# Two mixture-of-experts stages in a twelve-stage fp32 kernel: three of four token groups go from every expert to their two chosen ones, by sorted blocks and indexed transfers

## The chip, the core and the metric

The kernel runs on one core of a Trainium2 chip. The time is the device time of one launch, in microseconds (us). Engines are named as in the profile: PE (matrix products), DVE, ACT and POOL (element-wise work, POOL also issues indexed transfers), SP (issues DMAs). Names that end in q are the queues that feed them.

## The reference, cut to what matters

The state x has 2 x 1024 tokens of 128 numbers. Twelve stages in a row each add to x a function of its layer norm: L0 ffn, L0 attention, L0 ffn, L1 ffn, L1 attention, L1 ffn, L2 ffn, L2 attention (a time mixing of two layers), L2 ffn, L3 ffn, L3 attention, L3 ffn. The change is mainly about the two L1 ffn stages, called the L1 mixtures here:

```python
scores = xf @ gate_w                                   # 2048 tokens, 8 experts
top_v, top_i = jax.lax.top_k(scores, TOP_K)            # TOP_K = 2
probs = jax.nn.softmax(top_v, axis=-1)
combine = jnp.zeros((t, e), dtype=xf.dtype).at[jnp.arange(t)[:, None], top_i].add(probs)
h = jax.nn.gelu(jnp.einsum('td,edf->etf', xf, w1) + b1[:, None, :], approximate=False)   # 128 -> 512
y = jnp.einsum('etf,efd->etd', h, w2) + b2[:, None, :]                                   # 512 -> 128
out = jnp.einsum('etd,te->td', y, combine)
```

Six of eight entries in a row of `combine` are zero. The L2 and L3 mixtures have the same form with 256 in place of 512.

## The kernel before

x stays in SBUF the whole time as 16 tiles of 128 tokens; four tiles make a group (`NG` = 4 groups). The program of each engine is written stage after stage by hand, with semaphores between them; nothing is scheduled by a tool. All weights are in SBUF before the mixtures start, except those of L3, which SP loads into L1's place once the second L1 mixture is over (`late`).

**A mixture** (`moe_tensor`, `moe_scalar`, `moe_vector`) loops over groups, in them over the 8 experts, and in them over `nf` slices of the hidden width (4 in L1, 2 in L2 and L3). One turn of the innermost loop is a unit. PE computes a 128 x 512 hidden slice for 512 tokens (L394, two records in the trace), ACT applies the activation (L452), PE multiplies the four token tiles back (L409, eight records). After an expert's last slice DVE adds the result, scaled by the token's entry of `combine`, to x (L496). An L1 mixture has 4 x 8 x 4 = 128 units, every token through every expert.

**Joints.** A stage needs the norm of its input: statistics (L130, L231), normed rows (L250), four transposes by PE (L257), a copy (L265). Where a mixture is followed by anything, groups 0 to 2 of the next stage's norm are computed while groups 1 to 3 still run in the mixture; a mixture that follows a mixture (`early`) has nothing but its last group's front left to do. After an attention stage, the mixture does the whole front at its start. `keep_busy` (L1566) gives PE products of zeros, whose result nobody reads; before, it stands in both L0 ffn stages.

**L0 attention.** `values` clears PSUM bank 7 with one product of zeros (L2125) in each of its 32 phases, and then adds to it.

## Time and profile before

| what | value |
|---|---|
| time, median of 3 runs (lowest, highest) | 2359.88 us (2352.35, 2361.74) |
| profiled execution: its time, its span | 2360.02 us, 2358.0 us |
| mean granted TensorE clock | 0.965 |
| busy share of the span: PE, DVE, ACT, POOL | 92%, 63%, 45%, 6% |
| DMA traffic | 32.60 MB |

The span is the time from the first to the last instruction; 2.0 us lie around it. PEclk in a window is the granted clock of PE as a share of 2.4 GHz: 1.00 is 2.4 GHz, 0.50 is 1.2 GHz.

### The profile page before, as it was taken

How to read it: one execution, taken by the hardware profiler on the slowest of the kernel's cores; microseconds unless marked ns; L12 is line 12 of the kernel's file. 1: busy time of each engine (PE TensorE's matmuls, PEld its weight loads, DVE VectorE, ACT ScalarE, POOL GpSimd, SP SyncE). 2: the span in 40 equal slices, each digit the busy share in tenths (PEclk: the TensorE clock that was granted, in tenths of full speed). 3: DMA queues.
4: the chain of work that ended last, by engine and by line, in shares of the span. 5: the costliest groups of instructions: out<-in, count | busy, mean ns of one | idle time of the engine just before them, and what ended most of it. 6: DMA issues, size and time to landing. Idle time of an engine off the chain costs nothing.

```text
span 2358.0 us, 39152 instructions
## 1 busy us (share of the span) xinstructions
PE 2167.7 (92%) x13685; PEld 1350.0 (57%) x13723; DVE 1488.0 (63%) x4322; ACT 1060.1 (45%) x1816; POOL 134.3 (6%) x268
## 2 busy tenths in 40 slices
PE   7999999998999989999999987999998599998698
PEld 4423333336777656666666655777675367675476
DVE  6778888857433466666666664444456645777776
ACT  4257676663443345555555543433332233442133
POOL 2261111110000000000000000000000000000000
PEclk9989999999999999999999997999999789999899
DMA  6200000000000000000000000000100000000000
GB/s 215 66 25 27 26 25 25 24 21 3 1 1 1 1 1 1 1 0 0 0 0 0 0 1 1 1 1 1 57 1 1 0 1 1 1 1 1 1 1 19
DMA packets 22650, 32.60 MB, mean 14 GB/s; under 512 B 5768, under 2 KB 14233, under 8 KB 21756
## 3 DMA queue, kind: packets, MB, share of 16 engines
q1 hardware_dynamic: 21244, 29.81, 3.9%
q0 software_dynamic: 704, 0.85, 0.3%
q8 instruction: 77, 1.26, 0.2%
q10 hardware_dynamic: 576, 0.26, 0.1%
q14 instruction: 49, 0.40, 0.1%
HBM read 24.30 MB, written 5.24 MB: 13 GB/s over the span
## 4 chain that ended last, share of the span: by engine, by line
PE 81%; DVE 9%; issue 4%; ACT 4%; DMA 1%; SPq 1%; POOL 0%; ACTq 0%; DVEq 0%; POOLq 0%
PE ps L409 19%; PE ps L394 19%; PE ps L639 6%; PE ps L2130 5%; PE ps L605 5%; PE ps L2094 5%; PE ps L2115 4%; PE ps L622 3%; PE ps L589 2%; DVE x L821 1%; ACT arena L741 1%; PE ps L335 1%; PE ps L651 1%; PE ps L611 1%; PE ps L257 1%
## 5 line engine op out<-in xcount | busy, mean ns | idle before, releaser
L409 PEld LDWEIGHTS ps<-l_w,arena 128*128 128x128 f32 x4096 | 543.3, 194 | 261.7 <-issue 245.8
L409 PE MATMUL ps<-l_w,arena 128*128 128x128 f32 x4096 | 546.6, 278 | 12.0 <-DVE x L496 10.2
L394 PE MATMUL ps<-xnT,l_w 128*128 128x512 f32 x1024 | 536.6, 608 | 3.0 <-ACT xnT L265 3.0
L496 DVE SCALAR_TENSOR_TENSOR x<-ps,comb,x 128x128 f32<-128x128 f32 x768 | 216.4, 344 | 374.7 <-PE ps L409 372.5
L452 ACT ACTIVATE arena<-ps,l_b 128x512 f32<-128x512 f32 x384 | 263.6, 687 | 411.0 <-PE ps L394 410.8
L2380 DVE TENSOR_REDUCE arena<-ps 128x1 f32<-128x512 f32 x512 | 326.3, 685 | 46.3 <-PE ps L2094 46.3
L2285 ACT ACTIVATE arena<-ps 128x1024 f32<-128x1024 f32 x256 | 252.6, 1022 | 108.7 <-PE ps L2115 108.0
L803 DVE TENSOR_REDUCE arena<-ps 128x1 f32<-128x128 f32 (+7 forms) x256 | 178.7, 750 | 158.5 <-PE ps L611 158.5
L749 ACT ACTIVATE arena<-ps 128x512 f32<-128x512 f32 (+1 forms) x192 | 85.5, 489 | 250.5 <-PE ps L622 250.4
L741 ACT ACTIVATE arena<-ps,arena 128x128 f32<-128x128 f32 (+7 forms) x256 | 187.0, 745 | 13.5 <-DVE arena L803 13.5
L2094 PE MATMUL ps<-arena 72*128 72x512 bf16 x512 | 184.5, 389 | 1.6 <-DVE arena L2380 1.1
L394 PEld LDWEIGHTS ps<-xnT,l_w 128*128 128x128 f32 x1024 | 159.3, 196 | 15.8 <-issue 11.2
L622 PE MATMUL ps<-ident,arena 128*128 128x128 f32 x1152 | 159.8, 275 | 1.9 <-ACT arena L749 1.7
L605 PE MATMUL ps<-arena 64*128 64x512 f32 (+3 forms) x768 | 148.6, 506 | 12.2 <-ACT arena L741 10.7
L2115 PE MATMUL ps<-arena 75*128 75x512 bf16 x512 | 155.1, 386 | 3.3 <-DMA arena<-arena 3.3
L639 PE MATMUL ps<-arena 128*64 128x256 f32 (+1 forms) x1280 | 138.6, 363 | 19.0 <-DVE x L821 18.0
L622 PEld LDWEIGHTS ps<-ident,arena 128*128 128x128 f32 x1152 | 129.1, 142 | 39.1 <-ACT arena L749 29.9
L488 DVE SCALAR_TENSOR_TENSOR x<-l_b,comb,x 128x128 f32<-128x128 f32 x512 | 145.8, 347 | 4.2
L2094 PEld LDWEIGHTS ps<-arena 72*128 72x128 bf16 x512 | 50.0, 98 | 166.6 <-DVE arena L2380 118.5
L452 ACT ACTIVATE arena<-ps 128x512 f32<-128x512 f32 x128 | 76.4, 597 | 146.8 <-PE ps L394 146.5
L2130 PE MATMUL ps<-arena,xn 128*9 128x512 f32 x1024 | 135.6, 602 | 4.7 <-issue 0.2
L639 PEld LDWEIGHTS ps<-arena 128*64 128x64 f32 x1280 | 87.2, 137 | 65.8 <-issue 29.5
(389 smaller groups left out, 2023.5 us busy)
## 6 DMA issues: line engine op xcount, KB each, us to landing
l_w<-in_l_w SPq DMA_DIRECT2D x2, 2048.0 KB, 14.1
l_w<-in_l_w SPq DMA_DIRECT2D x4, 1024.0 KB, 12.6
arena<-s_parts_q SPq DMA_DIRECT2D x28, 144.0 KB
arena<-s_parts_k SPq DMA_DIRECT2D x28, 144.0 KB
s_parts_q<-arena SPq DMA_DIRECT2D x6, 256.0 KB, 3.3
s_parts_k<-arena SPq DMA_DIRECT2D x2, 768.0 KB, 5.0
arena<-arena SPq DMA_DIRECT2D x96, 2.0 KB
x<-in_x SPq DMA_DIRECT2D x4, 256.0 KB, 5.3
```

What stands on the lines that cost most here:

```text
L394: pe.matmul(k.ps[:, n % 2, :], w.w1[:, e, f * P:(f + 1) * P], k.xnT[:, g * GW:(g + 1) * GW], start=True, stop=True).then_inc(s.hidden_mm.s ...
L409: ins = pe.matmul(k.ps[:, 2 + e % 4, j * P:(j + 1) * P], w.h[:, n % 2, j * P:(j + 1) * P], w.w2[:, e, f, :], start=(f == 0 and j == 0), st ...
L452: act.activation(w.h[:, n % 2, :], k.ps[:, n % 2, :], s.func, **kw).then_inc(s.hidden.sem, 1)
L496: ins = dve.scalar_tensor_tensor(k.x[:, t, :], k.ps[:, 2 + e % 4, j * P:(j + 1) * P], k.comb[:, t, e:e + 1], k.x[:, t, :], ALU.mult, ALU.add)
L605: pe.matmul(k.ps[:, 2 * h + i + c // GW, 0:n], s.q[rows, b, qt * P:(qt + 1) * P], s.kT[rows, b, c:c + n], start=True, stop=c + n < width, ...
L622: ins = pe.transpose(k.ps[:, 4 + i, j * P:(j + 1) * P], s.p[:, 2 * (u % 2) + h, at + j * P:at + (j + 1) * P], k.ident[:, :])
L639: ins = pe.matmul(k.ps[64 * h:64 * h + 64, 6, at:hi], s.v[:, b * TB + kt, 64 * h:64 * h + 64], s.pT[:, h, kt, at:hi], start=(kt == 0), sto ...
L2094: pe.matmul(k.ps[:, bank, :], s.stack[0:s.ROWS, slot, 0, qt * P:(qt + 1) * P], s.stack[0:s.ROWS, slot, 1, half * GW:(half + 1) * GW], star ...
L2115: ins = pe.matmul(k.ps[:, 3 + 2 * (kt % 2) + h, :], s.stack[rows, slot, 1, kt * P:(kt + 1) * P], s.stack[rows, slot, 0, h * GW:(h + 1) * G ...
L2130: ins = pe.matmul(k.ps[at:at + s.DH + 1, 7, :], s.vs[:, place, 2 * m + odd, :], s.pT[:, 2 * m + odd, h * GW:(h + 1) * GW], start=False, st ...
L2285: act.activation(s.pT[:, kt, :], k.ps[:, bank:bank + 2, :].rearrange("p a b -> p (a b)"), ACT.Exp)\
L2380: dve.tensor_reduce(s.nm2[:, place, qt, half:half + 1], k.ps[:, bank, :], AX.X, ALU.max, negate=True)\
```

## The change

In both L1 mixtures only the first group of 512 tokens still goes through all experts. While it runs, the other 1536 tokens are sorted by chosen expert:

- SP writes the normed rows of groups 1 to 3 to DRAM (`l1_x_rows`). DVE makes masks of the first and second choice. PE counts, by 13 products against triangular and full matrices of ones (`sparse_prefix`, after unit 10), how many earlier tokens chose each expert; DVE turns this into a place for each of the 3072 choices (`sparse_places`), every expert's share padded to whole blocks of 128. That makes 31 blocks whatever the data are. 24 products (`sparse_index`, after unit 18) turn places into a list: for each row of each block a source row, a destination row and a weight.
- POOL gathers the 31 blocks from DRAM by 31 indexed transfers. SP reads each block's expert number out of SBUF into a register and loads that expert's w1, w2 and b1 (256 + 256 + 2 KB) into one of three slots of a ring; the slot of block b is free once block b-3 has been multiplied back.
- For each block PE transposes it, computes 4 products of 128 x 128 (`up`), ACT the gelu in 4 pieces, PE 4 products back (`down`), DVE scales by the weight and adds 4 pieces of the bias b2 to x, and POOL scatters the block to DRAM (`l1_y_rows`) by an indexed transfer.
- When all 31 have landed, SP reads the rows back, two per token, in six transfers, and DVE adds them and takes the statistics.

A stage after an L1 mixture therefore can't begin its norm of groups 0 to 2 during the mixture. For the L1 attention the mixture does it after the adds; the first L2 mixture is no longer `early`, and does the whole front itself.

Besides, `keep_busy` now stands at the start of each mixture that isn't `early` (40 products of zeros), before the second layer of the time mixing (36) and before the last products of the L3 attention (12), and no longer in the second L0 ffn; in the L0 attention the first real product of a phase starts the sum, and the clearing product is there in the first phase alone. Semaphores are shared between stages (no step is added by that).

```diff
-    def __init__(self, k, n, nf, func, w, gate, early):
+    def __init__(self, k, n, nf, func, w, gate, early, sparse=False):
         self.norm = Norm(k, n)
+        groups = self.groups = 1 if sparse else NG
...
+        keep_busy(pe, k, s.idle_bank, 40)
         front_turn(pe, k, s.norm, 0)
     hidden(0)
...
-    for n in range(NG * S):
+    for n in range(s.groups * S):
         g, i = divmod(n, S)
         e, f = divmod(i, nf)
-        if n + 1 < NG * S:
+        if n + 1 < s.groups * S:
...
+            if s.sparse is not None and i == s.sparse.PREFIX_UNIT:
+                sparse_prefix(pe, k, s.sparse)
+            if s.sparse is not None and i == s.sparse.INDEX_UNIT:
+                sparse_index(pe, k, s.sparse)
...
+    T0, TS = GT, NT - GT
+    TOKENS = TS * P
+    CHOICES = 2 * TS
+    BLOCKS = (2 * TOKENS + NE * (P - 1)) // P
+    RING = 3
+    PACKS = (BLOCKS + GT - 1) // GT
+    PREFIX_UNIT, INDEX_UNIT = 10, 18
...
+def sparse_sync(sp, k, m, s):
+    w, rows = s.w, s.w.x_rows[1:1 + s.TOKENS, :].rearrange("(t p) d -> p t d", p=P)
+    sp.wait_ge(k.consts, 8)
+    for g in range(1, NG):
+        sp.wait_ge(m.norm.rows.sem, m.norm.rows.at(g + 1))
+        if g == 1:
+            sp.dma_start(w.x_rows[0:1, :], k.zeros[0:1, 0:2 * D].bitcast(F32)).then_inc(s.stored.sem, 16)
+        sp.dma_start(rows[:, (g - 1) * GT:g * GT, :], k.xn[:, g * GT:(g + 1) * GT, :]).then_inc(s.stored.sem, 16)
+    sp.wait_ge(s.listed.sem, s.listed.at(s.EXPERTS))
+    for b in range(s.BLOCKS):
+        r, filled = b % s.RING, s.filled[b % s.RING]
+        if b >= s.RING:
+            sp.wait_ge(s.down_mm.sem, s.down_mm.at(b - s.RING + 1))
+        e = sp.value_load(s.experts[0:1, b:b + 1], min_val=0, max_val=NE - 1)
+        sp.dma_start(s.ring[:, r, 0:4 * P], w.w1_in[:, bass.ds(e, 1), :].rearrange("p a f -> p (a f)"))\
+            .then_inc(filled.sem, 16)
+        sp.dma_start(s.ring[:, r, 4 * P:], w.w2_in[:, bass.ds(e, 1), :, :].rearrange("p a f d -> p (a f d)"))\
+            .then_inc(filled.sem, 16)
+        sp.dma_start(s.b1[:, r, :], w.b1_in[:, bass.ds(e, 1), :].rearrange("p a f -> p (a f)"))\
+            .then_inc(filled.sem, 16)
+    sp.wait_ge(s.scattered.sem, s.scattered.at(16 * s.BLOCKS))
+    back = w.y_rows[1:1 + 2 * s.TOKENS, :].rearrange("(c t p) d -> c p t d", c=2, p=P)
+    for g in range(NG - 1):
+        tiles = slice(g * GT, (g + 1) * GT)
+        for c in range(2):
+            sp.dma_start(s.y_rows[:, c, tiles, :], back[c][:, tiles, :]).then_inc(s.y_in[g].sem, 16)
...
+    pool.wait_ge(s.stored.sem, s.stored.at(16 * NG))
+    pool.wait_ge(s.listed.sem, s.listed.at(s.INDEX))
+    for b in range(s.BLOCKS):
+        pool.indirect_dma_start(s.xg[:, b, :], None, s.w.x_rows,
+                                bass.IndirectOffsetOnAxis(ap=s.src[:, b:b + 1], axis=0))\
+            .then_inc(s.gathered[b // (2 * GT)].sem, 16)
+    for b in range(s.BLOCKS):
+        pool.wait_ge(s.y_out.sem, s.y_out.at(b + 1))
+        pool.indirect_dma_start(s.w.y_rows, bass.IndirectOffsetOnAxis(ap=s.dst[:, b:b + 1], axis=0), s.yb[:, b, :], None)\
+            .then_inc(s.scattered.sem, 16)
...
+def sparse_prefix(pe, k, s):
+
+    C = (s.TS + 1) * NE
+    flat = s.M.rearrange("p t e -> p (t e)")
+    pe.wait_ge(s.made.sem, s.made.at(8))
+    pe.wait_ge(s.listed.sem, s.listed.at(s.MASKS))
+    pe.matmul(k.ps[:, 7, 0:C], s.below, flat, start=True, stop=False, skip_group_check=True)
+    for t in range(s.TS):
+        ins = pe.matmul(k.ps[:, 7, (t + 1) * NE:C], s.ones, s.M[:, t, :].unsqueeze(1).broadcast_to([P, s.TS - t, NE]),
+                        start=False, stop=(t == s.TS - 1), skip_group_check=True)
+    ins.then_inc(s.listing.sem, 1)
...
+    for q in range(3):
+        at = slice(q * C // 3, (q + 1) * C // 3)
+        dve.tensor_tensor(s.marks[:, at, :], s.lane_of[:, at].unsqueeze(2).broadcast_to([P, C // 3, P]),
+                          s.lane.unsqueeze(1).broadcast_to([P, C // 3, P]), ALU.is_equal).then_inc(s.listed.sem, 1)
...
+def sparse_index(pe, k, s):
+
+    C, n = s.CHOICES, s.BLOCKS
+    for i in range(C):
+        if i % (C // 3) == 0:
+            pe.wait_ge(s.listed.sem, s.listed.at(max(s.MARKS[3 * i // C], s.PLACES)))
+        ins = pe.matmul(k.ps[:, 7, P:P + 2 * n], s.marks[:, i, :], s.rhs[:, i, :], start=(i == 0), stop=(i == C - 1),
+                        skip_group_check=True)
+    ins.then_inc(s.listing.sem, 1)
...
+    def up(b):
+        filled = s.filled[b % s.RING]
+        pe.wait_ge(s.xT_out.sem, s.xT_out.at(b // GT + 1))
+        pe.wait_ge(filled.sem, filled.at(48 * (b // s.RING + 1)))
+        if b < 2:
+            pe.wait_ge(m.hidden.sem, m.hidden.at(m.units - 1 + b))
+        else:
+            pe.wait_ge(s.hidden.sem, s.hidden.at(b - 1))
+        for f in range(4):
+            ins = pe.matmul(k.ps[:, b % 2, f * P:(f + 1) * P], s.ring[:, b % s.RING, f * P:(f + 1) * P],
+                            s.xT[:, b * P:(b + 1) * P], start=True, stop=True)
+        ins.then_inc(s.up_mm.sem, 1)
+
+    def down(b):
+        pe.wait_ge(s.hidden.sem, s.hidden.at(b + 1))
+        if b < 4:
+            pe.wait_ge(m.y_used.sem, m.y_used.at(NE - 3 + b))
+        else:
+            pe.wait_ge(s.y_out.sem, s.y_out.at(b - 3))
+        for f in range(4):
+            ins = pe.matmul(k.ps[:, 2 + b % 4, 0:D], m.w.h[:, b % 2, f * P:(f + 1) * P],
+                            s.ring[:, b % s.RING, (4 + f) * P:(5 + f) * P], start=(f == 0), stop=(f == 3))
+        ins.then_inc(s.down_mm.sem, 1)
...
+    pe.wait_ge(m.logits_out.sem, m.logits_out.at(1))
+    pe.wait_ge(s.listed.sem, s.listed.at(s.INDEX))
+    rows_in(0)
+    rows_in(1)
+    up(0)
+    for b in range(s.BLOCKS):
+        if b + 1 < s.BLOCKS:
+            up(b + 1)
+        if b % GT == 1 and b // GT + 2 < s.PACKS:
+            rows_in(b // GT + 2)
+        down(b)
...
+    todo = [(e, t) for e in range(NE) for t in range(s.T0, NT)]
+    for b in range(s.BLOCKS):
+        if b % GT == 1 and b // GT + 2 < s.PACKS:
+            turned(b // GT + 2)
+        dve.wait_ge(s.down_mm.sem, s.down_mm.at(b + 1))
+        dve.tensor_scalar(s.yb[:, b, :], k.ps[:, 2 + b % 4, 0:D], s.gate[:, b:b + 1], None, ALU.mult)\
+            .then_inc(s.y_out.sem, 1)
+        for e, t in todo[4 * b:4 * b + 4]:
+            ins = dve.scalar_tensor_tensor(k.x[:, t, :], m.w.b2[:, e, :], k.comb[:, t, e:e + 1], k.x[:, t, :],
+                                           ALU.mult, ALU.add)
+        if 4 * b < len(todo):
+            st.done(ins)
+    for g in range(1, NG):
...
+    for g in range(1, NG):
+        tiles = slice((g - 1) * GT, g * GT)
+        x = k.x[:, g * GT:(g + 1) * GT, :]
+        dve.wait_ge(s.y_in[g - 1].sem, s.y_in[g - 1].at(32))
+        st.done(dve.tensor_tensor(x, x, s.y_rows[:, 0, tiles, :], ALU.add))
+        dve.tensor_tensor(x, x, s.y_rows[:, 1, tiles, :], ALU.add).then_inc(s.added.sem, 1)
+        dve.wait_ge(s.added.sem, s.added.at(g))
+        ins = token_stats(dve, k, g)
+    st.done(ins)
+    if isinstance(m.nxt, Causal):
+        front_stats(dve, st, k, 0, NG - 1)
+        for g in range(NG - 1):
+            front_rows(dve, k, m.nxt.norm, g)
...
+            keep_busy(pe, k, 0, 36)
             norm_tensor(pe, k, s.norms[i])
...
+    keep_busy(pe, k, 5, 12)
     for g in range(NG):
...
-    keep_busy(pe, k, 3, 30)
+    if s.first:
+        keep_busy(pe, k, 3, 30)
...
             pe.wait_ge(s.vg, n + 1)
-            if not first:
+            if first:
+                pe.matmul(k.ps[:, 7, :], k.zeros[:, 0:P], k.zeros[:, :], start=True, stop=True)
+            else:
                 pe.wait_ge(s.oT_used, n)
...
         for h in range(s.QH):
             for odd in range(2):
                 at = 32 * (2 * h + odd)
                 ins = pe.matmul(k.ps[at:at + s.DH + 1, 7, :], s.vs[:, place, 2 * m + odd, :],
-                                s.pT[:, 2 * m + odd, h * GW:(h + 1) * GW], start=False, stop=(m == TB // 2 - 1),
+                                s.pT[:, 2 * m + odd, h * GW:(h + 1) * GW], start=(m == 0), stop=(m == TB // 2 - 1),
                                 tile_position=(0, at), skip_group_check=True)
...
-            early = NG - 1 if last is not None and last[0] == "moe" else 0
+            early = NG - 1 if last is not None and last[0] == "moe" and last[1].sparse is None else 0
             if name == "l1ffn":
-                stages.append(("moe", Moe(k, f"s{n}", 4, ACT.Gelu, L1w, "lin", early)))
+                stages.append(("moe", Moe(k, f"s{n}", 4, ACT.Gelu, L1w, "lin", early, sparse=True)))
```

The PE queue at the end of the first group of the first L1 mixture, before and after. Before, the next group's units follow (`l_w` are the weights in SBUF, `arena` the hidden values):

```order
L394 MATMUL ps<-xnT,l_w 128x512 [waits moe_hidden]
L409 MATMUL ps<-l_w,arena 128x128 [waits moe_hidden]
L409 MATMUL ps<-l_w,arena 128x128 x3
```

After, the blocks follow (L750 are transposes of gathered rows, L762 `up`, L773 `down`; `sparse_in0` to `sparse_in2` are the three ring slots, `gathered0` the first eight gathers):

```order
L417 MATMUL ps<-l_w,arena 128x128 x3
L750 MATMUL ps<-ident,arena 128x128 [waits gathered0,sparse_listed,moe_logits_out]
L750 MATMUL ps<-ident,arena 128x128 x7
L762 MATMUL ps<-arena 128x128 [waits moe_hidden,sparse_in0,xT_ready]
L762 MATMUL ps<-arena 128x128 x3
L762 MATMUL ps<-arena 128x128 [waits moe_hidden,sparse_in1,xT_ready]
L762 MATMUL ps<-arena 128x128 x3
L773 MATMUL ps<-arena 128x128 [waits moe_y_used,moe_hidden]
L773 MATMUL ps<-arena 128x128 x3
L762 MATMUL ps<-arena 128x128 [waits moe_hidden,sparse_in2,xT_ready]
```

So `up` of block b+1 stands ahead of `down` of block b, and each `up` waits for its ring slot.

SP's queue in that stage after the change, for one block from the fourth on (`moe_y_mm` counts the finished `down`s; the rows marked ISA are register operations); before, SP has nothing at all between the second L0 ffn and the loads of L3:

```order
L608 TENSOR_LOAD arena [waits moe_y_mm]
L608 ISA x2
L609 ISA
L609 DMA arena<-in_l_w 128x512
L611 DMA arena<-in_l_w 128x512
L613 ISA
L613 DMA arena<-in_l_b 128x4
```

These seven rows stand 28 times in each L1 mixture, after three times without the wait.

POOL's queue in the same stage, after; before, it holds only the three copies (L565 to L567) at the end of these rows:

```order
L644 DMA arena<-l_x_rows,arena 128x128 [waits sparse_listed,rows_stored]
L644 DMA arena<-l_x_rows,arena 128x128 x30
L649 DMA l_y_rows<-arena 7041x128 [waits moe_y_used] x31
L902 COPY arena<-l1a_wq 128x128 [waits sparse_added,l1_loaded]
L903 COPY arena<-l1a_wk 128x128
```

All gathers stand ahead of the first scatter.

## Rows read from the trace of the kernel before

**Rows 1.** Part 4 of the page: the chain that ended last, shares by engine
```profile
PE 81%; DVE 9%; issue 4%; ACT 4%; DMA 1%; SPq 1%; POOL 0%; ACTq 0%; DVEq 0%; POOLq 0%
```

**Rows 2.** The chain, one steady unit of the L1 mixture: start, duration, what
```profile
607.56 0.86 PE ps L394 x2
608.42 0.89 PE ps L409 x8
```

**Rows 3.** Timeline around the first L1 mixture: start, duration, what, xcount [idle before]
```profile
580.93 1.98 PE L394 MATMUL ps<-xnT,l_w 128*128 128x512 f32 x4 [0.75 <-ACT xnT L265]
...
816.90 5.37 PE L589 MATMUL ps<-xnT,arena 128*128 128x512 f32 x8 [2.04 <-POOL arena L566]
```

**Rows 4.** The chain through both L2 mixtures: start, duration, what
```profile
1678.59 1.72 PE ps L394 x4
...
1727.97 0.44 PE ps L257 x4
...
1873.33 3.41 PE ps L394 x4
...
1938.60 0.44 PE ps L257 x4
```

**Rows 5.** Timeline of PE where the two L1 mixtures begin
```profile
571.69 6.42 PE L1566 MATMUL ps<-zeros,ident_bf 128*128 128x512 bf16 x29 [0.16 <-issue]
...
579.56 0.63 PE L257 MATMUL ps<-ident,xn 128*128 128x128 f32 x4 [1.45 <-DVE xn L250]
595.74 1.57 PE L394 MATMUL ps<-xnT,l_w 128*128 128x512 f32 x2
...
1431.47 1.09 PE L257 MATMUL ps<-ident,xn 128*128 128x128 f32 x4 [10.68 <-DVE xn L250]
...
1451.87 2.06 PE L394 MATMUL ps<-xnT,l_w 128*128 128x512 f32 x2
```

**Rows 6.** Queue of SP: line L1913 (min/median/max ns), then one start-up load
```profile
L1913 SPq FUSED_REGOPS  x28: 37/56/75, 139.8 to 468.1; - x28
L1913 SPq DMA_DIRECT2D arena<-s_parts_q x28: 834/839/882, 140.4 to 468.3; - x28
...
11.03 0.43 SPq L2612 DMA_DIRECT2D l0a_wg<-in_l0a_wg  x1
```

**Rows 7.** DMA issues: queue, op, count, KB each, median us to landing
```profile
x<-in_x SPq DMA_DIRECT2D x4, 256.0 KB, 5.3
...
l_w<-in_l_wq SPq DMA_DIRECT2D x1, 64.0 KB, 1.8
...
arena<-x_rows,l_slot POOLq DMA_INDIRECT x2, 2.6
```

**Rows 8.** Windows, start-up loads: length, engines' busy time, PEclk, DMA share, GB/s
```profile
30.00:35.00 5.00, 5.00 (x13) 2.93 (x14) 1.98 (x9) 1.12 (x4) 0.00 (x0) 1.00 0.99 408
```

**Rows 9.** Timeline of POOL in the second L0 mixture
```profile
530.66 1.10 POOL L1372 DMA_INDIRECT arena<-x_rows,l_slot  x1 [13.77 <-DMA x_rows<-x]
532.06 0.97 POOL L1372 DMA_INDIRECT arena<-x_rows,l_slot  x1 [0.30 <-issue]
```

**Rows 10.** Windows of PE in the L2 time mixing: busy, PEclk, DMA share, GB/s
```profile
1856.00:1860.00 4.00, 2.02 (x16) 1.00 0.02 4
1864.00:1868.00 4.00, 0.00 (x0) 0.50 0.00 0
```

**Rows 11.** Line L2125, and a window of the L0 attention
```profile
L2125 PEld LDWEIGHTS ps<-zeros x32: 94/96/181, 130.7 to 508.4; 128*128 128x128 bf16 x32
...
240.00:290.00 50.00, 49.41 (x287) 15.72 (x291) 45.04 (x84) 35.12 (x38) 8.79 (x24) 1.00 0.08 26
```

**Rows 12.** Timeline of ACT and DVE: the sizes used for estimates
```profile
836.99 0.28 ACT L749 ACTIVATE arena<-ps 128x128 f32<-128x128 f32 x1 [4.20 <-PE ps L622]
...
574.59 1.17 DVE L231 BATCH_NORM_AGGREGATE small<-stat 128x2 f32<-128x6 f32 x16
578.30 4.18 DVE L250 TENSOR_SCALAR xn<-x,small 128x128 f32<-128x128 f32 x16
```

More of the change, by code:

```diff
@@ L445, in moe_scalar @@
         front_out(act, k, s.norm, 0)
-    for n in range(NG * S):
+    for n in range(s.groups * S):
         act.wait_ge(s.hidden_mm.sem, s.hidden_mm.at(n + 1))
@@ L479, in moe_vector @@
     moe_top(dve, st, k, s, s.early, NG, s.early)
+    if s.sparse is not None:
+        sparse_masks(dve, st, k, s.sparse)
     moe_gates(dve, st, k, s)
-    for g in range(NG):
+    for g in range(s.groups):
         for e in range(NE):
+            if s.sparse is not None and e == 1:
+                sparse_places(dve, st, k, s.sparse)
+            if s.sparse is not None and e == 2:
+                sparse_lists(dve, st, k, s.sparse)
             if w.b2 is not None:
@@ new lines, in sparse_tensor, with rows_in @@
+def sparse_tensor(pe, k, m, s):
+    def rows_in(c):
+        if c % 2 == 0:
+            come = s.gathered[c // 2]
+            pe.wait_ge(come.sem, come.at(16 * min(2 * GT, s.BLOCKS - c * GT)))
+        if c >= 2:
+            pe.wait_ge(s.xT_out.sem, s.xT_out.at(c - 1))
+        for j in range(s.pack(c)):
+            ins = pe.transpose(k.ps[:, 6 + c % 2, j * P:(j + 1) * P], s.xg[:, c * GT + j, :], k.ident[:, :])
+        ins.then_inc(s.xT_ps.sem, 1)
+    def up(b):
[33 more added lines that the diff above has]
+        for g in range(NG - 1):
+            if g == 2:
+                pe.wait_ge(m.nxt.norm.ready.sem, m.nxt.norm.ready.at(1))
+            front_turn(pe, k, m.nxt.norm, g, 6 + g % 2)
@@ new lines, in sparse_scalar @@
+def sparse_scalar(act, k, m, s):
+    for b in range(s.BLOCKS):
+        act.wait_ge(s.up_mm.sem, s.up_mm.at(b + 1))
+        if b < 2:
+            act.wait_ge(m.y_mm.sem, m.y_mm.at(m.units - 1 + b))
+        else:
+            act.wait_ge(s.down_mm.sem, s.down_mm.at(b - 1))
+        for f in range(4):
+            at = slice(f * P, (f + 1) * P)
+            ins = act.activation(m.w.h[:, b % 2, at], k.ps[:, b % 2, at], m.func, bias=s.b1[:, b % s.RING, f:f + 1])
+        ins.then_inc(s.hidden.sem, 1)
+    if isinstance(m.nxt, Causal):
+        for g in range(NG - 1):
+            front_out(act, k, m.nxt.norm, g, 6 + g % 2, **m.nxt.norm.affine)
@@ L1254, in __init__ @@
         self.ready = k.counted("xT_ready", NG)
-        self.stored = k.sem(f"{n}_stored")
-        self.gathered = [k.sem(f"{n}_gathered{m}") for m in range(self.MT)]
+        self.stored = k.counted("rows_stored", 0 if first else 16 * NG)
+        self.gathered = [k.counted(f"gathered{m}", 16) for m in range(self.MT)]
         self.spread = k.counted("l0_spread", 1)
@@ L1369, in l0moe_pool @@
     else:
[L1370 removed]
+        pool.wait_ge(s.stored.sem, s.stored.at(16 * NG))
     for m in range(s.MT):
@@ L2603, in build @@
         for w, _, _ in todo + late:
-            w.loads += 16
+            w.all.count += 16
         @block.sync
@@ L2648, in _ @@
             for kind, s in stages:
+                if kind == "moe" and s.sparse is not None:
+                    sparse_pool(pool, k, s, s.sparse)
                 if kind == "causal":
```

223 lines of the change are left out of this document (182 added, 41 removed).

## Prediction

> **What bounds the kernel now.** I read the page's chain first: 81% of the span is PE work [rows 1]. In the L1 mixture the chain is nothing but PE: 0.86 us for a hidden slice, 0.89 us for the four products back, 1.75 us for a unit [rows 2]. The stage runs from 580.93 to 816.90, 236.0 us [rows 3]; ACT and DVE wait for PE in it. Here removed PE work is removed time, until something else ends last. So I ask what will feed PE in the new stage: three ring slots filled by SP's queue, blocks gathered by POOL's, and a way out through DRAM. The trace has no such stage, only the pieces.
>
> **What is removed.** Three groups are 96 units, 168.1 us of PE in each L1 mixture.
>
> **What replaces it on PE.** 0.89 us is four products of 128 columns, so 0.22 us each. A block has eight (1.78 us) and a transpose (0.11): 1.9 us, 31 blocks 58.6 us. If PE set the pace, each mixture would win 109 us less its ends. I don't believe it does. What waits behind a late `up` is `down` of the block before it on PE's queue, so DVE's scaling, POOL's scatter and SP's refill of that slot all move with it.
>
> **The ring.** `up` of block b waits for its slot; the slot is refilled after `down` of b-3. With period P, from the start of `up` b to the end of `down` b passes P + 1.78 (the next `up` and this `down` are behind one period). Three periods are that plus the refill R: 3P = R + P + 1.78, so P = (R + 1.78)/2. R in steps:
> - the read of the expert number into a register, v. Nothing in the trace does this. Below, it costs no less than a register operation, 0.06 us [rows 6]; above, I take the quickest load from DRAM to landing, 1.8 us [rows 7]. It is a round trip, but needs no DMA: 1.0 us, near the middle.
> - register operations, waking: 0.3.
> - three loads. Issuing costs 0.43 us each at start-up with fixed addresses, 0.84 with an address from a register [rows 6]. The bytes, 512 KB at 408 GB/s [rows 8], take 1.3 us on top of some 1.8 for a small one [rows 7]: 3.1; and the third, begun after two issues (0.9 to 1.7), lands 1.8 later: 2.7 to 3.5. I take 3.5, since these addresses come from registers.
>
> R = 4.8, P = 3.3 us. SP itself needs v + 0.3 + three issues, 2.6 to 3.8 us a block: it hardly fits in the period, and may be the bound. With all ends low (v 0.06, loads 3.1) P = 2.6; with all high SP is busy 1.8 + 0.3 + 2.5 = 4.6 us. So P is 2.6 to 4.6, and 1 us of P is worth 2 x 28 = 56 us. This one term makes the range.
>
> The Trainium skill ("Runtime: NRT & Kernel Launch", the preamble breakdown) gives about 1.3 us for a register load from DRAM at launch. With it for v, P would be 3.45 and the forecast 8 us later; ours reads SBUF, and no row here shows either.
>
> What is hidden in a period of 3.3 us: ACT's four pieces, at most 0.28 us each by the nearest row [rows 12], 1.1; DVE's five pieces at 0.26 (a sixteenth of 4.18, [rows 12]), 1.3, and a share of the transposes' copies. If P fell to 1.9, DVE would be near the bound. POOL takes 1.4 us for an indexed transfer from issue to issue [rows 9]: 31 gathers 43 us, 31 scatters the same, below P. The gathers' start: 13 units, 22.8 us, lie behind the list products, a microsecond of them goes to DVE's list, and eight gathers need 8 x 1.4 + 1.5 = 12.7. Hidden, with 9 us to spare; sixteen need 23.9, and PE wants them some 4 us into the blocks, at about 26: just in time.
>
> **One L1 mixture, after.** First group: before, 236.0 less the last 2.0 of idle time, less 168.1 and the successor's three groups of transposes (0.44 each, [rows 4]) is 64.6. Added: 13 + 24 products at 0.22 = 8.1, and 2 for a lower clock behind so many narrow ones, as behind the gate's (1.57 us at 595.74 for what takes 0.86 later, [rows 5, 2]). DVE's some 30 operations on lists fall into the time it idles. 74.7. Filling the pipe up to the first `down`: 4.9 (8 transposes 0.9, copy 0.7, two `up`s 1.8, ACT's rest 0.6, `down` 0.9). Two blocks at 1.9 and 28 at 3.3: 96.2. End of the last `down`: 175.8.
>
> **Its tail**, wholly exposed: scale 0.3, scatter 2.6 [rows 7], six reads of 256 KB. Four such in flight land after a median 5.3 [rows 7]; the sixth about 9. Last adds and statistics about 2.2. 14.1. Then the front, from the aggregation at 574.59 to the first product at 580.93: 6.3 [rows 12, 3]. The L1 attention wants two more groups, 1.05 each on DVE: 22.5 in all for it, 20.4 for the L2 mixture.
>
> **First L1 mixture**: 236.0 - (175.8 + 22.5 + 1) = **-36.7**, with 1 for colder first products.
>
> **Second L1 mixture with the L2 mixture's opening.** Before: 1678.59 - 1433.30 (= 1431.47 plus turn and copy, 1.83) = 245.3; of it 4.2 are a cold start, booked at the joints: 241.1. After: 175.8 + 20.4, plus what an L2 mixture costs without `early`. The trace has both kinds: up to the first transposes for its successor the early one takes 1727.97 - 1678.59 = 49.4, the other 1938.60 - 1873.33 = 65.3 [rows 4]. 15.9 more. 241.1 - 212.1 = **-29.0**. The 40 products of zeros there run right behind the last `down` (8.8 us at 0.22, [rows 5]), while the tail lasts 20: they are over long before and save nothing.
>
> **Joints.** At the second L1 mixture PE idles 10.68 us; 40 products take 8.8. From first transpose to the product behind the gate: cold 20.40, warm 16.18 [rows 5], so -4.2. At the second L2, the L3 and the two inner places I allow -5.5 together: there less is cold, and two fillers are longer than the idle time they fill. At the first L1 mixture 40 instead of 30 end at 580.4, 0.8 after the transposes could start (579.56): +0.7. **-9.0**.
>
> **L0 attention.** 31 products of zeros less at 0.22 = 6.8. PE is 49.41 of 50 us busy there, DVE 45.04 [rows 11], so nothing else takes over: **-6.5**.
>
> Sum: -36.7 - 29.0 - 9.0 - 6.5 = -81.2. 2358.0 - 81.2 = 2276.8, plus 2.0 around the span: **2279 us**. The profiled execution (2360.02) is at the median (2359.88), so no correction.
>
> **Rivals.**
> - *The clock falls while PE waits.* At P = 3.3 PE is busy 57% of the time in bursts. For: after 4 us with nothing the clock was 0.50. Against: in the window before, half busy, it was still 1.00 [rows 10]. At 0.50 a block's products take 3.56, P = (4.8 + 3.56)/2 = 4.2: 50 us later, 2329. The Trainium skill ("TensorE: Matmul & The Clock Gate", the part on oscillation) tells of a kernel whose short bursts between DMA waits each started cold, which would speak against this change. Chance 0.13.
> - *SP is the bound*, at 4.0 to 4.6: 2318 to 2352. Chance 0.12.
> - *Slower than before: register reads and addresses cost more than any row here.* Place: SP's seven rows between two blocks. It decides from P = 3.3 + 81/56 = 4.75, which needs v above 1.95 with 0.84 for each issue; at v = 2.5, SP takes 5.3 and the kernel 2391. Nothing in the trace excludes it, since v is not in it. Chance 0.07.
> - *The ring doesn't bind*: PE paces at 1.9 to 2.3 us. It needs R below 2.8, less than the bytes and one landing. 2201 to 2223. Chance 0.05.
> - *The gathers hold PE up*: 31 in a row may go slower than two did. From 1.55 us each the second eight are late; at 2.8, twice the row, by some 20 us in each mixture: 2319. It could join any case; 0.1, inside the forecast's range or just above it.
>
> The forecast, P from 2.6 to 3.9 with the other terms within 10 of their sum, has 0.63: 2235 to 2318. To leave out two in ten at most, the range goes on through the clock and most of SP's case: 2228 to 2346. About 0.5%, 12 us, is what a measurement can tell from no change. Faster by more (below 2348): 0.63 + 0.13 + 0.10 of SP's case + 0.05 = 0.91. Within: 0.02 of SP's case and 0.01 of the slower one; slower: 0.06.
>
> **What the profile would show.** L762 starting about 3.3 us apart, ended by a DMA of `l_w`; SP's queue 2.6 to 3.8 busy per block; PE about six tenths busy and PEclk 1.00 in that stretch; some 14 us without PE work between the last L773 and the front, apart from the fillers; about 200 us from the first L401 to the L1 attention's first product; L0 attention 6 us shorter. I am wrong above all if the register read or the issues are off, and, less, if the list operations of DVE come too late for unit 18, which stops PE and POOL in turn.

## The result, and the profile after

| | before | after |
|---|---|---|
| median (lowest to highest) | 2358.85 us (2352.35 to 2361.74) | 2320.69 us (2311.14 to 2328.06) |
| profiled execution, its span | 2360.02, 2358.0 | 2311.14, 2309.0 |

The ratio is 0.984, 95% interval 0.981 to 0.988: 38 us faster, where 81 were forecast. The profiled execution of the changed kernel is its quickest, so the two traces are 49.0 us apart. I account for these 49.0 first, then for the other 11. Two executions lie far above all others and are left out of every figure: 3833 us of the kernel with split waits, and 7607 us of the kernel before, beside the first four experiments.

| stretch, by the first transposes of its stage | before | after | measured | forecast |
|---|---|---|---|---|
| up to the first L1 mixture | 579.56 | 569.17 | -10.4 | -5.8 |
| first L1 mixture, to the L1 attention's value products (L586, now L923) | 242.5 | 218.5 | -24.0 | -36.7 |
| second L1 mixture with the L2 mixture's opening, to the L2 time mixing | 368.5 | 353.9 | -14.5 | -33.2 |
| the rest | | | -0.1 | -5.5 |

The page of the changed kernel (part 4, the chain by engine; part 5 for the blocks; part 6, the DMA issues):

```profile
PE 77%; DVE 9%; issue 7%; ACT 4%; DMA 2%; SPq 1%; ACTq 0%; DVEq 0%; POOL 0%; POOLq 0%
...
L762 PE MATMUL ps<-arena 128*128 128x128 f32 x496 | 79.6, 311 | 83.7 <-issue 79.5
...
arena<-in_l_w SPq DMA_DIRECT2D x124, 256.0 KB, 3.0
...
arena<-l_y_rows SPq DMA_DIRECT2D x12, 256.0 KB, 5.2
```

PE's share of the chain fell from 81% [rows 1] to 77%. `up` (L762) has 83.7 us of idle time before it. Without it PE would set the pace, but most of it was forecast: 3.3 less 1.9 us, 56 times, is 78. The page calls it "issue", since it finds no releaser. So I read the queues side by side. PE in the middle of the second mixture's blocks:

```profile
1522.75 1.13 PE L762 MATMUL ps<-arena 128*128 128x128 f32 x8 [2.65 <-issue]
1523.72 1.57 PE L773 MATMUL ps<-arena 128*128 128x128 f32 x8
1525.69 2.00 PE L762 MATMUL ps<-arena 128*128 128x128 f32 x8 [0.41 <-issue]
1527.52 1.05 PE L773 MATMUL ps<-arena 128*128 128x128 f32 x8
1530.01 1.13 PE L762 MATMUL ps<-arena 128*128 128x128 f32 x8 [1.43 <-issue]
1530.97 0.60 PE L750 MATMUL ps<-ident,arena 128*128 128x128 f32 x4
1531.41 1.06 PE L773 MATMUL ps<-arena 128*128 128x128 f32 x8
1533.49 1.13 PE L762 MATMUL ps<-arena 128*128 128x128 f32 x8 [1.02 <-issue]
```

and SP's queue in the same stretch:

```profile
1529.40 0.34 SPq L609 DMA_DIRECT2D arena<-in_l_w  x1
1529.83 0.38 SPq L611 DMA_DIRECT2D arena<-in_l_w  x1
1530.39 0.33 SPq L613 DMA_DIRECT2D arena<-in_l_b  x1
1533.21 0.34 SPq L609 DMA_DIRECT2D arena<-in_l_w  x1
```

A `down` ends at 1528.57 (1527.52 + 1.05). The first load for its slot is issued 0.83 later, the third 0.99 behind the first, and the `up` of that slot starts 3.10 behind the third. Together 4.92 us: this is R, in one example. The lines of that queue, with their durations in ns, and behind L609, L611 and L613 the time to landing in us:

```profile
L608 SPq TENSOR_LOAD <-arena x62: 262/268/497, 604.5 to 1585.8; - x62
L608 SPq FUSED_REGOPS  x62: 152/152/183, 605.0 to 1586.1; - x62
...
L609 SPq DMA_DIRECT2D arena<-in_l_w x62: 337/338/376, 605.5 to 1586.6; - x62
...
DMA to landing us min/median/max: 2.7/3.0/3.3
...
L611 SPq DMA_DIRECT2D arena<-in_l_w x62: 332/376/604, 605.9 to 1587.0; - x62
...
DMA to landing us min/median/max: 3.0/3.1/3.4
...
L613 SPq DMA_DIRECT2D arena<-in_l_b x62: 332/333/402, 606.5 to 1587.6; - x62
...
DMA to landing us min/median/max: 2.7/3.2/4.6
```

The register read costs 0.27 us, and a load with an address from a register 0.34 to 0.38, less than half of the row I had for one (0.84, [rows 6]). The loads land 3.0, 3.1 and 3.2 us after issue (medians); the last is the smallest, 2 KB of biases, in the queue behind 512 KB. `up` waits for all three. Over the 56 refills of both mixtures, the first load is issued 0.8 us behind the `down`, the third 1.0 behind the first, and `up` starts 3.35 behind the third.

From such rows I took two averages over the blocks of both mixtures in every run: R, from the end of a `down` to the `up` three blocks on, and X, from the start of an `up` to the end of the `down` behind it. In the changed kernel R is 5.2, X 2.4 (median 2.02) and the period P, from `up` to `up`, 3.8; the forecast had 4.8, 1.78 and 3.3. The mean of X is above its median since some blocks are cold: PE's granted clock is 1.2 instead of 2.4 GHz, and an `up` that is all cold takes 2.05 us from start to end instead of 1.13. In 14 of the 62 it takes over 1.2; these are called cold below. From the first `down`'s end to the last one's pass 108.5 and 111.2 us, where 96.2 were forecast. This is 12.3 and 15.0, 27 of the 32 missing us.

The tail came as forecast. DVE and SP behind the first mixture's blocks:

```profile
762.12 3.36 SPq L620 DMA_DIRECT2D arena<-l_y_rows  x6
766.01 0.69 DVE L836 TENSOR_TENSOR x<-x,arena 128x512 f32<-128x512 f32 x1 [6.44 <-DMA arena<-l_y_rows]
...
772.18 0.87 DVE L130 BATCH_NORM_STATS2 stat<-x 128x6 f32<-128x128 f32 x4
...
777.67 3.22 PE L257 MATMUL ps<-ident,xn 128*128 128x128 f32 x12 [18.48 <-DVE xn L250]
...
781.58 2.07 PE L926 MATMUL ps<-xnT,arena 128*128 128x512 f32 x2 [0.69 <-ACT xnT L265]
```

The last `down` ends at 759.18 and the L1 attention's first product starts at 781.58: 22.4 us against 22.5.

### The profile page after: what moved, and what is told of

Same layout as the page of the kernel before. It is cut to its first block, busy times and chain, and to the rows that moved or that the text cites. A ratio compares the mean times of both kernels' runs of the same rounds, so it can differ in the third digit from the quotient of the medians.

```text
span 2309.0 us, 38832 instructions
## 1 busy us (share of the span) xinstructions
PE 2049.9 (89%) x13192; PEld 1283.4 (56%) x13192; DVE 1477.2 (64%) x4188; ACT 999.5 (43%) x1872; POOL 262.5 (11%) x408
## 4 chain that ended last, share of the span: by engine, by line
PE 77%; DVE 9%; issue 7%; ACT 4%; DMA 2%; SPq 1%; ACTq 0%; DVEq 0%; POOL 0%; POOLq 0%
PE ps L417 12%; PE ps L401 12%; PE ps L976 6%; PE ps L2471 5%; PE ps L942 5%; PE ps L2434 5%; PE ps L2455 5%; PE ps L959 3%; PE ps L762 3%; PE ps L773 3%; PE ps L926 2%; DVE x L1158 1%; ACT arena L1078 1%; PE ps L1905 1%; PE ps L988 1%
## 5 line engine op out<-in xcount | busy, mean ns | idle before, releaser
L417 PEld LDWEIGHTS ps<-l_w,arena 128*128 128x128 f32 x2560 | 344.7, 196 | 174.4 <-issue 164.5
L417 PE MATMUL ps<-l_w,arena 128*128 128x128 f32 x2560 | 347.2, 280 | 14.4 <-DVE x L518 12.6
L401 PE MATMUL ps<-xnT,l_w 128*128 128x512 f32 x640 | 342.1, 619 | 3.7 <-ACT xnT L265 3.7
L518 DVE SCALAR_TENSOR_TENSOR x<-ps,comb,x 128x128 f32<-128x128 f32 x576 | 162.2, 345 | 147.0 <-PE ps L417 144.9
L466 ACT ACTIVATE arena<-ps,l_b 128x512 f32<-128x512 f32 x192 | 131.7, 687 | 226.1 <-PE ps L401 225.8
L762 PE MATMUL ps<-arena 128*128 128x128 f32 x496 | 79.6, 311 | 83.7 <-issue 79.5
L804 ACT ACTIVATE arena<-ps,arena 128x128 f32<-128x128 f32 x248 | 70.9, 368 | 163.7 <-PE ps L762 163.7
```

The lines of the kernel that those rows point to most:

```text
L401: pe.matmul(k.ps[:, n % 2, :], w.w1[:, e, f * P:(f + 1) * P], k.xnT[:, g * GW:(g + 1) * GW], start=True, stop=True).then_inc(s.hidden_mm.s ...
L417: ins = pe.matmul(k.ps[:, 2 + e % 4, j * P:(j + 1) * P], w.h[:, n % 2, j * P:(j + 1) * P], w.w2[:, e, f, :], start=(f == 0 and j == 0), st ...
L466: act.activation(w.h[:, n % 2, :], k.ps[:, n % 2, :], s.func, **kw).then_inc(s.hidden.sem, 1)
```

## The experiments

Theory A is the ring: P = (R + X)/(slots - 1), and what lies between a `down` and the landing that `up` waits for is worth half of its length in each period. Theory B is the bytes: 514 KB a block set the period. Theory C is the clock: PE is cold in part of the stretch, and that is why P is 3.8 and not 3.3. Given that blocks follow each other evenly, the formula only adds up intervals. What can fail is that R stays where it is when the slots change, and that P follows when a part of R is cut. The expectations of the first four runs still took X as 1.78 and put all of the excess of P on R (5.9); by the averages above R is 5.2 and X 2.4.

**One load less.** DVE builds the biases of all blocks from the resident table, as a product with a one-hot of the expert numbers and a sum:

```diff
-        sp.dma_start(s.b1[:, r, :], w.b1_in[:, bass.ds(e, 1), :].rearrange("p a f -> p (a f)"))
-            .then_inc(filled.sem, 16)
...
+    st.done(dve.tensor_tensor(own, s.ahead.unsqueeze(2).broadcast_to([P, n, 4, NE]),
+                              s.w.b1[:, 0:4 * NE].rearrange("p (e f) -> p f e", f=4)
+                              .unsqueeze(1).broadcast_to([P, n, 4, NE]), ALU.mult))
+    st.done(dve.tensor_reduce(s.b1.rearrange("p b f -> p (b f)"), own.rearrange("p b f e -> p (b f) e"), AX.X, ALU.add))
```

> The third load of a block (2 KB of biases) is gone: DVE picks all 31 blocks' biases out of the resident table before the blocks begin, four operations in time that it idles. Theory A (the way from the end of a `down` to the last landing sets the period, P = (R + 1.78)/2, with R 5.9 in the trace of the changed kernel): the last landing is then that of the second weights, issued 0.4 instead of 1.0 us behind the first and landing 3.0 instead of 3.2 us after its issue, so R falls by some 0.8, P from 3.85 to 3.45, and the kernel by 56 x 0.4 = 22 us, to about 2298. Theory B (the bytes, 512 KB a block, set it): 2 of 514 KB are gone, no change, 2320. Theory C (the clock, lower in part of the stretch, sets it): no change or a few us.

Measured: 2298.3 us (2289.7 to 2307.5), ratio to before 0.975 [0.971, 0.979]: 2 KB out of 514 bring 22 us, the time that A forecast. The mechanism was there in part only. The last load is issued 0.6 us earlier, but `up` starts 3.65 behind it instead of 3.35, so R fell by 0.3 (5.2 to 4.9) and not by 0.8, and P by 0.2 to 3.6, which is 12 us between these two traces. Some of that is X, 2.4 to 2.25, so this run alone doesn't exclude C.

**Waits split.** The three loads are as before, but each counts on a semaphore of its own:

```diff
 def up(b):
-        pe.wait_ge(filled.sem, filled.at(48 * (b // s.RING + 1)))
+        pe.wait_ge(filled.sem, filled.at(16 * (b // s.RING + 1)))
...
 def down(b):
+        come = s.filled2[b % s.RING]
+        pe.wait_ge(come.sem, come.at(16 * (b // s.RING + 1)))
...
 # sparse_scalar
+        come = s.filled3[b % s.RING]
+        act.wait_ge(come.sem, come.at(16 * (b // s.RING + 1)))
```

> The three loads stay, in the same order, but each is waited for by its own reader: `up` waits for the first weights alone, ACT for the biases, `down` for the second weights. Theory A: `up` is released about 0.9 (end of `down` to the first issue) + 3.0 (landing) = 4.0 us after `down`, so P is (4.0 + 1.78)/2 = 2.9 where neither biases nor second weights come later than their readers; biases land some 1.2 us later than the first weights, `up` takes 0.9, so ACT may wait 0.3: P 2.9 to 3.1, 42 to 53 us less, 2268 to 2279. Theory B (bytes): the queues still carry the same bytes in the same order, so little changes, 2310 to 2320. Theory C (clock): little changes.

Measured: 2272.8 us (2270.5 to 2276.9), ratio 0.965 [0.962, 0.968]. R 4.2, P 3.2, just above the 2.9 to 3.1 expected. The same bytes in the same order, and 48 us less: B is out. All that changed is which landing holds which reader.

**No register read.**

```diff
-        e = sp.value_load(s.experts[0:1, b:b + 1], min_val=0, max_val=NE - 1)
+        e = b % NE
```

This kernel leaves out which expert a block belongs to: block b takes the weights of expert b mod 8, as many bytes as before.

> SP's read of the expert number and the address made from it are left out: block b loads the weights of expert b mod 8, so the blocks' results are those of wrong experts; all else is the same. Theory A: 0.27 for the read and about 0.2 of register work before the first load, some 0.1 before each other: R falls by 0.5 to 0.7, P by 0.25 to 0.35, 14 to 20 us, 2301 to 2307. If the read costs much more than its row in the trace shows (waking the queue, a hidden wait), P falls by more than 0.5: below 2293. Theories B and C: no change, 2320.

Measured: 2287.6 us (2283.6 to 2297.3), ratio 0.971 [0.967, 0.975], 33 less than the changed kernel. That is below 2293, the mark set for a read that costs more than its row. The traces tell the size. From the end of a `down` to the first issue pass 0.03 us instead of 0.78, and the three issues stand 0.1 closer, so the read with its register work took 0.9 and not the expected 0.5 to 0.7. A part came back: `up` starts 3.6 behind the third issue instead of 3.35. R fell from 5.2 to 4.5 and P from 3.8 to 3.4, and the spans are 19 us apart; against the repeat below (R 5.35, P 4.0) they are 34 apart. How much of the 33 is the read and how much the changed kernel's own spread stays open between these two.

**Without the blocks.** All groups go through all experts; fillers, L0 attention and shared semaphores as changed:

```diff
-                stages.append(("moe", Moe(k, f"s{n}", 4, ACT.Gelu, L1w, "lin", early, sparse=True)))
+                stages.append(("moe", Moe(k, f"s{n}", 4, ACT.Gelu, L1w, "lin", early)))
```

> All four groups go through all experts again; what is left of the change are the products of zeros at the joints, the clearing products taken out of the L0 attention, and the shared semaphores. From the difference of the two traces up to the first L1 mixture (10.4 us) and behind the second L2 mixture's start (none): 2348. By the prediction's terms (L0 attention -6.5, joints -9.0): 2343 to 2345. The joints' part is right if the first hidden slices behind the filler are no longer cold.

Measured: 2348.4 us (2342.3 to 2350.8), ratio 0.996 [0.994, 0.998]. So some 10 us of the 38 (5 to 14 by the interval) have nothing to do with the blocks, as the two traces had led to expect and less than the prediction's terms. By its trace, 10.7 us shorter, L0 is 4.0 us shorter and the opening of the second L1 mixture, from its first transposes to the product behind the gate, 4.2 (16.21 us); the rest is 2.5 in all.

**Four slots.**

```diff
-    RING = 3
+    RING = 4
...
+        self.slots = [ring[:, i, :] for i in range(3)] + [more[:, i, :] for i in range(2)]
```

> One size is changed: four ring slots instead of three, the fourth in columns of the arena that this mixture doesn't use. Theory A: by the trace of the changed kernel R is 5.2 on average and from the start of an `up` to the end of the `down` behind it pass 2.0 warm, 2.4 on average; four slots give P = (5.2 + 2.2)/3 = 2.5 instead of 3.8, 27 blocks twice: 70 us less, about 2250. Theory B (the 514 KB of a block set the period): no change, 2320. SP as the bound (about 1.9 us of rows a block) would show only below 2.3.

Measured: 2240.4 us, ratio 0.951 [0.949, 0.954]: 80 us less than the changed kernel. R is 5.7, X 2.2, P 2.6. R grows by half a microsecond: 0.2 before the first issue and 0.3 behind the third, at more bytes per microsecond in the queues. A gives the rest.

**Five slots, one load less.** `RING = 5`, the fifth slot in the other half of `more`, together with the first experiment's edit.

> Five slots and no third load (DVE picks the biases ahead). Theory A: (5.0 + 2.0)/4 = 1.75, less than what PE itself takes (1.9 to 2.0) and DVE (five pieces at 0.35 and a share of a copy, 1.9), so P is 2.0 to 2.3 and the kernel 84 to 100 us below the changed one: 2220 to 2236. The ring no longer sets the end; the next bound is DVE or PE, which the waits show. Theory B: no change.

Measured: 2212.3 us (2205.3 to 2212.7), ratio 0.938 [0.936, 0.940], some 8 us below the expected 2220 to 2236. P is 2.1, as expected. The run changes two things, and doesn't say how much each is worth. PE in the second mixture's blocks:

```profile
1451.73 1.06 PE L769 MATMUL ps<-arena 128*128 128x128 f32 x8
1452.62 1.06 PE L780 MATMUL ps<-arena 128*128 128x128 f32 x8
1453.52 1.06 PE L769 MATMUL ps<-arena 128*128 128x128 f32 x8
1454.41 1.06 PE L780 MATMUL ps<-arena 128*128 128x128 f32 x8
```

and a window over most of them (PE, PEld, DVE, ACT, POOL busy, then PEclk, DMA share, GB/s):

```profile
1435.00:1490.00 55.00, 50.96 (x439) 49.40 (x438) 35.72 (x120) 29.78 (x106) 34.54 (x35) 1.00 0.88 284
```

`up` (L769) and `down` (L780) follow each other without idle time, at 0.89 us each; DVE, of which I was wary, is busy 65%. PE is the bound now. The queues carry 284 GB/s, where the changed kernel has about 160: bytes were never near their limit at three slots.

**Zeros in the gaps.**

```diff
             pe.wait_ge(s.hidden.sem, s.hidden.at(b - 1))
+            if b >= s.RING:
+                keep_busy(pe, k, b % 2, 5)
+        pe.wait_ge(filled.sem, filled.at(48 * (b // s.RING + 1)))
```

> The changed kernel with five products of zeros (1.1 us warm) ahead of each `up` from block 3 on, in the time that PE waits for the ring anyway (1.3 us on average). It tells how much the lower clock in part of the stretch costs: if X (start of `up` to the end of the `down` behind it) is 2.0 everywhere, P falls by 0.2, some 10 us; where a gap is shorter than 1.1 us the zeros delay `up`, which takes part of it back: 2308 to 2322. Theory C (the clock is the main reason for 3.8 instead of 3.3): 28 us or more less, below 2292.

Measured: 2310.5 us (2310.0 to 2316.2), ratio 0.981 [0.979, 0.983], whose interval overlaps the changed kernel's 0.984 [0.981, 0.988]. Cold `up`s fell from 14 of 62 to 5, and X to 2.2. But R rose to 5.4: what the clock gives back, the zeros take, and P is 3.8 as in the changed kernel's first trace. C as the main reason is out, since that wanted 2292 or less. As a part it stays: by the formula the lower clock is worth some 9 us (see the next section), and this run can't show them. With the zeros in between, the view of groups by line also names what `up` (here L764) waits for:

```profile
L764 PE MATMUL ps<-arena 128*128 128x128 f32 x496 | 71.9, 291 | 37.6 <-DMA arena<-in_l_b 33.3 <-DVE arena L818 4.1
```

Of 37.6 us of idle time the landing of the 2 KB load (`in_l_b`) ends 33.3.

**Other fillers at two joints.**

```diff
-        keep_busy(pe, k, s.idle_bank, 40)
+        if s.after_sparse:
+            pe.wait_ge(*s.free)
+        keep_busy(pe, k, s.idle_bank, s.fill)
```

`s.fill` is 50 behind the L1 attention and 27 behind the second L1 mixture, where the filler also waits for the tail's last add.

> The changed kernel with other fillers at two joints: 50 instead of 40 products of zeros before the second L1 mixture (11.0 us for an idle time of 10.7), and before the first L2 mixture 27 that wait for the last add of the tail, so that they run up to the transposes instead of ending 10 us before. If the opening is cold because the filler ends too early: -3 to -4 at each, 2312 to 2314. If zeros don't help there: 2320 or, where 50 are too long, 1 us more.

Measured: 2311.3 us (2306.6 to 2317.2), ratio 0.981 [0.979, 0.983], near the expected 2312 to 2314, but not told apart from the changed kernel's 0.984 [0.981, 0.988]. The openings did get warm. Before the second L1 mixture, in the changed kernel,

```profile
1386.39 8.81 PE L1905 MATMUL ps<-zeros,ident_bf 128*128 128x512 bf16 x40
1397.07 0.66 PE L257 MATMUL ps<-ident,xn 128*128 128x128 f32 x4 [1.87 <-DVE xn L250]
1398.47 3.78 PE L401 MATMUL ps<-xnT,l_w 128*128 128x512 f32 x4 [0.75 <-ACT xnT L265]
```

and with 50:

```profile
1386.82 10.74 PE L1907 MATMUL ps<-zeros,ident_bf 128*128 128x512 bf16 x49 [0.16 <-issue]
1397.39 0.60 PE L257 MATMUL ps<-ident,xn 128*128 128x128 f32 x4
1398.74 1.98 PE L401 MATMUL ps<-xnT,l_w 128*128 128x512 f32 x4 [0.75 <-ACT xnT L265]
```

3.78 became 1.98, and the same at the L2 mixture. In this trace the blocks took 5 us more than in the changed kernel's, and the spans are alike (2309.8 and 2309.0).

**Best of these together.** Five slots, one load less, these fillers.

> Five slots, biases picked by DVE, and the fillers of the joints run put together. In the five-slot run PE already paces the blocks (2.1 us), so only the openings are left to gain: 3.5 at the second L1 mixture and about 4 at the first L2 mixture. 2203 to 2207.

Measured: 2213.5 us (2210.4 to 2216.9), ratio 0.939 [0.937, 0.941]. The fillers add nothing that can be measured to the five slots; the expectation of 5 to 9 us more was wrong. In its trace the stretch from the first L2 mixture's first transposes to its successor's is 5.3 us shorter, L0 3.1 longer, and the second L1 mixture 0.1 shorter.

**The changed kernel once more.**

> The changed kernel itself once more, beside the other runs, since its first four runs spread from 2311 to 2328 us and the profiled one was the quickest. If that spread is its own (the clock in the blocks, which differs from run to run), the median is again 2315 to 2325.

Measured: 2320.4 us (2310.8 to 2325.6), ratio 0.984 [0.981, 0.986]. Its profiled execution is the slowest of the five, 2325.6 us, and the first one was the quickest, so the two show what the spread is made of: L0 ends 6.7 us later, and first `up` to last `down` takes 118.7 and 120.5 us instead of 113.0 and 115.7. R is 5.35, X 2.6, and 21 of 62 `up`s are cold. Windows of PE within the first mixture's blocks (busy, PEclk, DMA share, GB/s), first the changed kernel's, then its repeat's:

```profile
676.20:691.20 15.00, 10.34 (x71) 0.89 0.52 154
691.20:706.20 15.00, 8.98 (x75) 1.00 0.56 159
706.20:721.20 15.00, 9.32 (x69) 0.91 0.55 158
721.20:736.20 15.00, 9.17 (x73) 0.97 0.60 170
```

```profile
683.00:698.00 15.00, 8.92 (x71) 1.00 0.57 170
698.00:713.00 15.00, 11.04 (x67) 0.77 0.48 143
713.00:728.00 15.00, 9.92 (x68) 0.89 0.52 148
728.00:743.00 15.00, 9.81 (x67) 0.89 0.49 140
```

The granted clock differs from execution to execution.

**Half the bytes.**

```diff
-        sp.dma_start(s.ring[:, r, 0:4 * P], w.w1_in[:, bass.ds(e, 1), :].rearrange("p a f -> p (a f)"))
+        sp.dma_start(s.ring[:, r, 0:2 * P], w.w1_in[:, bass.ds(e, 1), 0:2 * P].rearrange("p a f -> p (a f)"))
```

and the second weights likewise.

> Only half of each weight block is loaded (two loads of 128 KB instead of 256), and the products use that half twice, so the blocks' results are wrong; number and order of the instructions are the same. By the prediction's term (1.3 us for the bytes of 512 KB on top of the landing of a small load) R falls by 0.65 and P by 0.3: 17 to 20 us less, about 2300. Theory B (bytes set the period) would have P fall by half of 3.8: below 2230. If the landing doesn't depend on the bytes: 2320.

Measured: 2284.2 us (2278.5 to 2288.3), ratio 0.970 [0.967, 0.972], 36 less than the changed kernel and 16 less than expected. R is 4.35 and P 3.3, so 256 KB are worth 0.8 to 1.0 us of a landing, where the forecast's term made it 0.65. The bytes lengthen the landing; they don't set the period, or P would have halved. The products use each half of the weights twice.

**Two slots.**

> Two slots instead of three. The formula gives P = R + X = 5.2 + 2.1 to 2.4 = 7.3 to 7.6 us instead of 3.8; less where R falls because SP is never behind (4.9): 7.0. 29 blocks twice: 185 to 220 us more, 2505 to 2540, slower than before the change.

Measured: 2600.2 us, one run, where 2505 to 2540 were expected. P is 8.8, not 7.3 to 7.6. PE and a window of it:

```profile
704.42 2.05 PE L762 MATMUL ps<-arena 128*128 128x128 f32 x8 [5.02 <-issue]
706.26 1.91 PE L773 MATMUL ps<-arena 128*128 128x128 f32 x8
713.08 2.04 PE L762 MATMUL ps<-arena 128*128 128x128 f32 x8 [4.90 <-issue]
714.91 1.92 PE L773 MATMUL ps<-arena 128*128 128x128 f32 x8
```

```profile
680.00:695.00 15.00, 4.76 (x21) 0.61 0.26 79
```

R is 4.95 as ever; X is 3.8, nearly twice its warm 2.03: behind some 5 us of waiting 61 of the 62 `up`s are cold, at the lower level, 1.2 GHz. My expectation had kept X at the three-slot value.

All runs in one table (us, averages of both mixtures in the profiled execution):

| run | slots | R | X | P | kernel |
|---|---|---|---|---|---|
| changed, first profile | 3 | 5.2 | 2.4 | 3.8 | 2320.7 |
| changed, repeat | 3 | 5.35 | 2.6 | 4.0 | 2320.4 |
| one load less | 3 | 4.9 | 2.25 | 3.6 | 2298.3 |
| waits split | 3 | 4.2 | 2.15 | 3.2 | 2272.8 |
| no register read | 3 | 4.5 | 2.3 | 3.4 | 2287.6 |
| half the bytes | 3 | 4.35 | 2.25 | 3.3 | 2284.2 |
| zeros in the gaps | 3 | 5.4 | 2.2 | 3.8 | 2310.5 |
| two slots | 2 | 4.95 | 3.8 | 8.8 | 2600.2 |
| four slots | 4 | 5.7 | 2.2 | 2.6 | 2240.4 |
| five slots, one load less | 5 | 6.3 | 2.1 | 2.1 | 2212.3 |

With five slots R is no longer a refill but the wait for PE's own turn. The two profiles of the changed kernel are near its quickest and its slowest execution, so a difference is best read against their middle: R 5.25, X 2.5, P 3.9.

## Why the prediction was off

The sign, the bound and the mechanism were right: three slots hold PE up, a refill by SP sets the period, and the kernel gets faster by less than the products removed. The gain was half of the forecast: 38 us instead of 81, and 49.0 between the traces. The time lies in the stated range, 3 us above the part that had 0.63. The step that failed is the size of one term, the ring's period. These are the terms in turn:

- **The ring's period**, 3.3 against 3.8 in the profile (4.0 in the repeat). It is worth 27 of the missing 32 us between the traces, and the formula was not at fault, its inputs were, X more than R. *X*: I used 1.78, eight times the pace of a product. From start to end warm blocks take 2.03 (0.97 + 1.06), which is 0.12 of P. In 12 of 60 four transposes stand between `up` and `down`, 0.44 us, which the formula had left out: 0.05. A lower clock in part of the blocks brings the average from 2.1 to 2.4, 0.15 of P, about 9 us; in the repeat to 2.6, about 14. *R*: 5.2 instead of 4.8, 0.2 of P. Within R two errors partly cancelled, and that R came out so near is luck. The read and what goes with it were too dear: 1.3, where the first load was issued 0.8 after the `down` on average. The three loads were too cheap: 3.5, where they took 1.0 + 3.35 = 4.4. I took the third one's landing as that of a small load on its own, 1.8 [rows 7]; in the queue behind 512 KB it is 3.2. The run with one load less, the one with split waits and the waits named in the run with zeros show that this landing was what `up` waited for.
- **Joints**, -9.0 forecast. At the second L1 mixture 40 products end 1.87 us early and the opening is cold: 19.97 from first transposes to the product behind the gate, 20.40 before, -0.4 instead of -4.2. Without the blocks the same filler gave all of the 4.2, and with 50 products the same; so the size was right and whether it comes depended on the clock. The others give -0.1 instead of -5.5 together. The allowance for them was a guess, and the runs don't bear it out: at the last L3 mixture the opening is 1.75 shorter (gate products 12.57 instead of 14.32 behind the transposes), while the L2 time mixing with its new filler takes 1.1 more.
- **L0**, -5.8 forecast, -10.4 in the profile, -3.7 in the repeat and -4.0 without the blocks. The forecast lies within this spread.
- **First group** (first hidden slice to the first `down`'s end, 79.6 forecast, 80.2 measured), **tail** (22.5 and 22.4; 20.4 and 20.6), and **the L2 mixture without `early`** (65.3 to its successor's transposes; 64.0) were right.

By rivals: *the clock falls while PE waits* had its chance at 0.13, as the whole half-clock case. In truth it comes in single blocks: 14 and 21 of 62 in the two profiles, 1.00 in some windows and 0.77 in others, where the prediction had written 1.00 for the whole stretch. The Trainium skill ("TensorE: Matmul & The Clock Gate", oscillation) describes bursts that each start cold between DMA waits. The two-slot run agrees (61 of 62 `up`s cold behind some 5 us of waiting), the three-slot one only in part. *SP is the bound*: no, its rows fill some 1.7 us of 3.8 (0.27 + 0.15 + 0.34 + 0.38 + 0.33, and 0.2 of small ones). *Register reads too dear*: no, 0.27 for the read and 0.75 with all that stands between the `down` and the first issue. The Trainium skill ("Runtime: NRT & Kernel Launch", the preamble breakdown) gives about 1.3 us for its register loads from DRAM; this one, of one number from SBUF, takes a fifth, so adding that figure would have brought the total nearer by accident only. *The ring doesn't bind*: not at three slots; at five it doesn't. *The gathers hold PE up*: 1.25 us apart, all 31 issued by 662.5, and the transposes of the gathered rows have no idle time before them.

The other 11 us, between the traces' 49 and the medians' 38, are what the profiled execution was quicker than its kernel's median (9.6), and what the one before was slower (1.2). The repeat shows where such differences arise: L0 and the clock in the blocks. What sets the clock in one execution rather than another stays open.
